# Third attention layer: head means taken from the weights, one norm for two, and gathers sixteen ahead

## What is computed

```python
x = x + _L2_xattn_ref(_layernorm(x, axis=-1), ctx_2048, ...)
...
ln_out = _ln(hidden_states, ln_w, ln_b)
q = _ln(fp8_linear(ln_out, wq, ...).reshape(b, s, g, hpg, d), qln_w, qln_b)   # 16 heads; qx likewise
k = _ln(fp8_linear(ln_out, wk, ...).reshape(b, s, g, d), kln_w, kln_b)        # 8 heads; kx from cond
v = fp8_linear(ln_out, wv, ...)                                               # no norm
core, xout = _gqa(q, k, v), _gqa(qx, kx, vx)
return (concat(core, xout) / smooth, rounded to fp8) @ wproj.T * scales
```

## Time and profile before

| what | value |
|---|---|
| median of 3 runs | 1890.64 us (1887.36 to 1892.12) |
| profiled execution | 1887.24 us, span 1885.5 us, mean PE clock 0.871 |
| busy in the span | PE 1544.3, DVE 1120.1, ACT 813.7, POOL 777.2 us |
| stages touched | l1f 601 to 868, its norms to 883, l2q to 922, main loop to 1350, l3f 1632 to 1885.5 |
| rows put back in l3f | first gather 1678.63, last scatter 1853.75 |

### The profile page before, as it was taken

How to read it: one execution, slowest core, us unless ns; L and a number is a source line. 1 busy time by engine, 2 the same in 40 slices (tenths; PEclk the granted TensorE clock), 3 DMA queues, 4 the chain that set the end, 5 groups by cost and what they waited for, 6 DMA issues and landing times. The chain is left out here.

```text
span 1885.5 us, 25460 instructions
## 1 busy us (share of the span) xinstructions
PE 1544.3 (82%) x8600; PEld 982.3 (52%) x8600; DVE 1120.1 (59%) x2581; ACT 813.7 (43%) x1887; POOL 777.2 (41%) x1038
## 2 busy tenths in 40 slices
PE   6566659999797899994499999999699989837772
PEld 5322225656464455653266676666556565525551
DVE  5999971223674533426789999999622255463335
ACT  2898863110333211113488888888521112412221
POOL 1276641000200497800578777777310000026772
PEclk9666558999697999997699999999799988858886
DMA  2298871110504013111100000000111100146646
GB/s 76 59 180 180 177 153 44 34 42 17 179 2 163 34 56 120 56 45 46 45 1 1 2 1 1 1 2 1 43 29 39 37 24 1 69 177 214 244 140 239
DMA packets 174225, 140.13 MB, mean 74 GB/s; under 512 B 141793, under 2 KB 154721, under 8 KB 170386
## 3 DMA queue, kind: packets, MB, share of 16 engines
q1 hardware_dynamic: 165314, 114.89, 21.4%
q0 software_dynamic: 6416, 22.03, 3.5%
q10 hardware_dynamic: 2368, 1.61, 0.3%
HBM read 85.43 MB, written 19.50 MB: 56 GB/s over the span
## 5 line engine op out<-in xcount | busy, mean ns | idle before, releaser
L1817 POOL CAST l0m_pi<-l0m_pf 128x1024 bf16<-128x1024 int16 x128 | 133.2, 1040 | 111.1 <-ACT l0m_pf L1884 109.6
L1420 PE MATMUL l2x_pr<-l_w,l2x_xq 128*128 128x512 bf16 x576 | 141.4, 384 | 40.0 <-ACT credits L42 40.0
L350 PE MATMUL l1e_gu<-x_normT,l1e_w 128*128 128x512 f32 x384 | 171.6, 601 | 0.0
L1884 ACT ACTIVATE l0m_pf<-l0m_s,l0m_bias,l0x_sq 128x1024 int16<-128x1024 f32 x128 | 153.9, 1204 | 18.7 <-DVE l0m_bias L1915 12.3
L1911 DVE TENSOR_REDUCE l0m_mx<-l0m_s 128x1 f32<-128x1024 f32 x128 | 155.5, 1215 | 5.5 <-PE l0m_s L1826 5.2
L1555 DVE TENSOR_SCALAR l2x_raw<-l2x_raw,l2x_mv,l2x_rs 128x128 f32<-128x128 f32 x384 | 141.7, 429 | 1.6 <-POOL l2x_rs L1399 1.5
L1826 PE MATMUL l0m_s<-l0x_kT,l0x_qT 64*128 64x512 bf16 x256 | 69.0, 559 | 68.5 <-ACT l0m_pf L1884 65.7
L350 PE MATMUL l0e_gu<-x_normT,l0e_w 128*128 128x512 f32 x272 | 121.2, 600 | 0.0
L350 PEld LDWEIGHTS l1e_gu<-x_normT,l1e_w 128*128 128x128 f32 x384 | 74.0, 194 | 84.3 <-issue 83.3
L350 PE MATMUL l2e_gu<-x_normT,l2e_w 128*128 128x512 f32 x256 | 114.5, 602 | 0.0
L426 DVE TENSOR_TENSOR l1e_h<-l1e_sil,l1e_gu 128x512 f32<-128x512 f32 x40 | 27.5, 686 | 133.0 <-ACT l1e_sil L402 133.0
(11 more groups left out here) (516 smaller groups left out, 3562.8 us busy)
## 6 DMA issues: line engine op xcount, KB each, us to landing
l3m_w<-in_l_moe SPq DMA_DIRECT2D x16, 1280.0 KB, 6.4
l1e_w<-in_l_ffn SPq DMA_DIRECT2D x24, 384.0 KB, 3.0
l_rows<-zero_row SPq DMA_DIRECT2D x8, 1024.0 KB, 11.0
l_w<-l_rows SPq DMA_DIRECT2D x8, 1024.0 KB, 11.8
l0e_w<-in_l_ffn SPq DMA_DIRECT2D x17, 384.0 KB, 3.0
l2e_w<-in_l_ffn SPq DMA_DIRECT2D x16, 384.0 KB, 3.1
ctx_tok<-l_route SPq DMA_DIRECT2D x8, 512.0 KB
l2q_wps<-in_l_wp SPq DMA_DIRECT2D x16, 256.0 KB, 2.8
```

The source lines that it names most:

```text
L350: last = nc.tensor.matmul(gu[half][:, m, :], w[:, c % SW, (2 * k + m) * P:(2 * k + m + 1) * P], pg.xnT[:, k, cols(n)], start=(k == 0), sto ...
L1420: last = nc.tensor.matmul(flat(pr[t % 2][:]), src[:, k, tokens], pg.l2_w3[:, part, k, at:at + W], start=(k == 0 and part == 0), stop=(k == ...
L1817: nc.gpsimd.tensor_copy(pi[:, n % 8, :], pf[:, n % 4, :]).then_inc(s["rounded"], 1)
L1884: nc.scalar.activation(pf[:, n % 4, :], s_ps[n % 3][:], ACT.Exp, scale=sq[:, b, h:h + 1], bias=bias[:, n % 4:n % 4 + 1], accum_out=sm[:, b ...
```

## The change

1. **Means out of the weights.** A head's mean over its 128 columns is linear in the weights, so the mean is taken from the weights once. In l1f, DVE runs a new function `beside` behind the multiplications of a chunk. In chunks 0 to 5 and 12 to 15 it sums 8 heads of a 128x1024 piece of `l2_raw` (a reduction) and divides by 128, into `l2_means`; from chunk 12 on it waits for the reload. In chunks 16 and 18 it does the same for the context's weights `l2_wx` and subtracts as well (128x1024). POOL's `l2_split` waits for each mean and scales with eight 128x128 operations that subtract and multiply, where it had one of 128x1024 that multiplied; V keeps the one.
2. **One norm for two.** `l2xm` goes; `l2xn` transposes and takes the factor of both (var x (1 + eps) + eps²).
3. **Rounding.** The subtraction of `l2q` moves from POOL to DVE.
4. **Main loop.** POOL's chain makes no mean, and its constants are folded: 6 operations and a power where there were 9 and a power. DVE multiplies four heads in one 128x512 product with the reciprocal roots broadcast, where it had four operations of 128x128. `aff` holds a factor sqrt(128) for the scales, and is filled by 8 tiny operations, where there were 4.
5. **Gathers.** `AHEAD` becomes 16, in memory that the third attention has left (`spent`); 8 gathers are issued up front, then a scatter and two gathers until 16 are ahead, then one and one, and 16 scatters at the end.

The core of the diff:

```diff
+def l2_centre(pg):
+    v, piece, heads = pg.nc.vector, 1024, 8
+    ch = Chain(None, pg.sem("l2_mean_steps"))
+    def beside(dve, c):
+        ch.eng = dve
+        def mean(dst, rows):
+            ch.link(v.tensor_reduce(dst, rows, AX, ALU.add))
+            return v.tensor_scalar(dst, dst, heads / piece, None, ALU.mult)
+        if c < 6 or 12 <= c < 16:
+            half, (i, k) = (0, divmod(c, KD)) if c < 6 else (1, divmod(c - 10, KD))
+            if half == 0:
+                dve.wait_ge(pg.l2_w_in, 16 * 3)
+            else:
+                dve.wait_ge(pg.l2_rest_in, 16)
+            rows = pg.l2_raw[:, k, i * piece:(i + 1) * piece].rearrange("p (h d) -> p h d", h=heads)
+            mean(pg.l2_means[:, half, k, i * heads:(i + 1) * heads], rows).then_inc(pg.l2_mean_in, 1)
+        elif c in (16, 18):
+            ...
+            ch.link(mean(dst, rows))
+            ch.link(v.tensor_tensor(rows, rows, dst.unsqueeze(2).to_broadcast([P, heads, piece // heads]), ALU.subtract))
+    return beside
...  l2_split
-                    ch.link(g.tensor_scalar(raw, raw, pg.l2_in_scale[:, c:c + 1], None, ALU.mult))
+                    if which == V_:
+                        ch.link(g.tensor_scalar(raw, raw, pg.l2_in_scale[:, c:c + 1], None, ALU.mult))
+                    else:
+                        centred += 1
+                        pool.wait_ge(pg.l2_mean_in, centred)
+                        for h in range(heads):
+                            at_h, m = at + h * P, at // P + h
+                            ch.add(g.tensor_scalar(pg.l2_raw[:, k, at_h:at_h + P], pg.l2_raw[:, k, at_h:at_h + P], pg.l2_means[:, half, k, m:m + 1],
+                                                   pg.l2_in_scale[:, c:c + 1], ALU.subtract, ALU.mult))
+                        ch.wait()
...  ffn_block, DVE, behind the multiplications of a chunk
+                if beside:
+                    beside(dve, c)
...  attention_l2
-    norm(pg, "l2xm", pg.xn)
...  l2q
-            @block.gpsimd
-            def _(pool):
-                for n, (k, j) in enumerate(jobs):
-                    pool.wait_ge(widened, n + 1)
-                    nc.gpsimd.tensor_tensor(xq[:, j, k, :], wide[:, n % 2], step[:, n % 2], ALU.subtract).then_inc(rounded, 1)
...
                     widen(nc, ch, z[:, u], step[:, u], wide[:, u]).then_inc(widened, 1)
+                    dve.wait_ge(widened, n + 1)
+                    nc.vector.tensor_tensor(xq[:, j, k, :], wide[:, u], step[:, u], ALU.subtract).then_inc(rounded, 1)
...  main loop, DVE
-                            for j in range(U):
-                                last = nc.vector.tensor_scalar(raw[:, u, j, :], raw[:, u, j, :], mv[:, u, j, 0:1],
-                                                               rs[:, 1, u, j:j + 1], ALU.subtract, ALU.mult)
-                            last.then_inc(s["normed"], 1)
+                            nc.vector.tensor_tensor(raw[:, u], raw[:, u], rs[:, 1, u].unsqueeze(2).to_broadcast([P, U, DH]), ALU.mult)\
+                                .then_inc(s["normed"], 1)
...  moe_l3
-    GROUP, LOADS, AHEAD, NY = 4, 6, 6, 4
+    GROUP, LOADS, AHEAD, FIRST, NY = 4, 6, 16, 8, 4
...
-            for e in range(AHEAD):
+            for e in range(FIRST):
                 gather(e)
             pool.wait_ge(pg.rows_zeroed, 16 * 8)
             for e in range(E):
                 scatter(e)
-                if e + AHEAD < E:
-                    gather(e + AHEAD)
+                for n in range(min(FIRST + 2 * e, e + AHEAD), min(FIRST + 2 * e + 2, e + AHEAD + 1)):
+                    if n < E:
+                        gather(n)
```

57 lines of the change are left out of this document (30 added, 27 removed).

## The result

The changed kernel takes 1843.41 us in the median of 4 runs (1840.65 to 1846.31), the kernel before 1889.19 in 4 runs beside it (1887.36 to 1892.12). The ratio is 0.9756, interval 0.9733 to 0.978: 46 us faster. The profiled execution took 1841.28 us (span 1839.5, mean PE clock 0.873).

What follows compares the result with a forecast made beforehand. PE was nearly the loop's bound, losing time to waits for DVE and POOL; POOL's indirect DMAs ordered l3f. Terms -15 - 6.5 - 4.6 + 0 - 9 = -35.1 led to 1855 us, own range 1847 to 1867, with rivals 1845 to 1871.

Steps and rivals of the forecast that it cites:

- Norms: Ahead of the main loop: one whole norm of 6.47 us goes, -6.5 us.
- l2q: Rounding ahead of the loop: subtraction on DVE, POOL idle, 35.05 us becomes 30.4, -4.6 us, ends 3.5 and 5.
- l1f: Stage before the norms: DVE's means and POOL's longer split steps fit in beside a busy PE, 0 us.
- the two bounds for the eight operations: POOL's split in l1f: 4.4 us by elements and starts, 7.3 at twice the elements' time; a step 12.9 to 15.8.
- rival C: l1f: POOL's split doesn't fit, ten steps ending too late above 21 us each; slower, 1905 us; 4%.
- l3f: Gathers and scatters: sixteen gathers ahead remove POOL's idle time, -9 us, ends -10 and 0.
- the ring of four outputs: l3f's tail: the last 16 scatters are bound by the experts, 1.63 us each, in four output slots.
- Rival B: l3f's tail: last 16 experts slower than POOL saves, 2.45 us each at lower PE clock, nothing gained, 1864; 12%.
- the term of -15: Main loop: PE's waits for DVE and POOL, 15.8 us, nearly all go; ends -18.5 and -6.
- their hidden part: Main loop: a real wait of PE exceeds the recorded one by 0.16 us, added for 16 and 10 waits.
- Rival A: Main loop gives nothing: product as slow as the four operations, or another engine sets the pace; 1870 us; 17%.
- Rival D: Main loop gives more than the recorded waits, losses over ACT and PE weight loads vanishing too; down to 1846; 7%.

Runs made afterwards that it cites:

- The kernel with two passes: The changed kernel with POOL's eight operations per step of the l1f split made twice, first subtraction, then scaling: 1855.56 us in one profiled run, l1f 290.22.
- The cross of the two: Three variants of the changed kernel: four plain scalings, POOL's chain at ten operations, four operations subtracting a zero mean; 1848.68, 1859.38 and 1873.14 us.
- before again: The kernel before, unchanged, run again: median 1887.51 us, ratio to before 1.0002.
- after again: The changed kernel, unchanged, run again: median 1840.15 us, ratio to before 0.9748.
- the kernel with ten operations and the product: The changed kernel with three more small operations in POOL's chain, result unread, the product kept: 1859.38 us in one profiled run, loop 418.8.

## Why the prediction was right or wrong

**Norms, right.** -6.5 predicted, -6.47 measured (from the norm's first statistics to DVE's first instruction of l2q 14.93 before, 868.23 to 883.16, and 8.46 after, 862.65 to 871.11).

**l2q, right.** A job takes 3.79 where 3.75 and a little for semaphores was reckoned, and the stretch shrinks by 4.52 instead of 4.6.

**l1f, right, with a wrong limit.** The stretch stays at 281.6, PE busy 205 of 205. A step on POOL takes 15.1 to 15.5, within 12.9 to 15.8, by the dearer of the two bounds for the eight operations (6.2 to 7.1 against 4.4 to 7.3). The first half ends at 740.9, the means wait for nothing, POOL ends at 838.7. But rival C's bound for the end, 21 us per step, was wrong: ten steps from 656 to 868 left out the reload, 12.4, and the two steps for V, 11.3 each. With them it is (868 - 656 - 12.4 - 22.6) / 10 = 17.7. The kernel with two passes, at 17.9 and with a slower reload, lost 8.6 us. The margin was some 2 us per step and not 6.

**l3f, right in the sum, wrong in the tail.** -9 was taken, the working gave 9.5, -9.8 was measured. Up to scatter 48, 144.2 us after the first gather (143.9 worked out), POOL had one pause of more than the usual 0.30 us between issues, 0.96 ahead of the first scatter. Behind it I let the ring of four outputs bind at 1.63 us each from expert 52 on. In fact the scatters went on 1.28 apart up to 57, and only the last six came 1.6 apart. Rival B, slow last experts, didn't come: they run at 1.6, not at 2.45.

**Main loop, wrong size and wrong cause.** This is the step that failed: the term of -15 from the marked waits of PE. The sum counted 15.8 and took 15; measured were 19.4, beyond the term's own end of 18.5. Cut at the first projection of the second batch and at that of the eighth, both by the context's weights, the start gave 1.8, six periods 13.1 (305.8 to 292.7), and the end 4.5. At start and end the recorded waits and their hidden part, 5.9 of the 15.8, stand against 6.3 measured. In the six periods they are 9.9, against 13.1: 0.5 us per batch was missing. It is in the timeline of before, in waits that carry no mark:

```profile
983.11 1.05 PE L1433 MATMUL l2x_s<-l2x_kT,l2x_qT 128*128 128x128 f32 x8
984.00 0.60 PE L1440 MATMUL l2x_tr<-ident,l2x_raw 128*128 128x128 f32 x4
...
995.72 1.05 PE L1433 MATMUL l2x_s<-l2x_kT,l2x_qT 128*128 128x128 f32 x8
996.85 0.66 PE L1447 MATMUL l2x_pt<-ident,x_norm 128*128 128x128 f32 x4
997.35 1.46 PE L1420 MATMUL l2x_pr<-l_w,l2x_xq 128*128 128x512 bf16 x6
```

From L1433 to the next group are 1.13 us at 995.72 and 0.89 undisturbed (983.11 to 984.00), and the disturbed group takes 0.50 to the next instead of 0.44. Neither has a bracket. One such gap, 0.24, and some 0.05 behind each of seven disturbed groups, 0.36 in all, make up the half microsecond or so. It was within reach: in after, and in undisturbed batches, PE's period is the sum of its own undisturbed steps, and those could be read in the trace of before: 1.67 at the three marked waits of that batch, 0.24 and 0.36, 2.27 in all, taken from 50.95 leave 48.68. The prediction came to 49.1, from the busy time and the marked waits.

The cause was wrong too. The prediction said that the product takes DVE off PE's way, and that POOL's three operations come on top. The cross of the two shows that neither is worth much alone (-5.2 and +3.2). DVE's share, 92%, and POOL's, 76%, are means over steps; in the steps without a pause both were above PE's 6.09. The 88 us less work on DVE were too much as well: 384 operations at a mean of 429 ns make 1.72 us per four only if they don't overlap, and the same row's busy time, 141.7, makes 1.48. Against the product's 78.3 that is 63 us less, and DVE's busy time in the whole loop fell by 51.6. That the sum came near was luck in so far: it rested on both waits going, and only the pair made them go. Rival A, in which another engine takes DVE's place and sets the pace, is close to what the product alone did: PE waited 0.3 us for DVE at the transposes and 11.4 for POOL.

**Rival D** named losses beyond the recorded waits and down to 1846, and that is what happened in the loop. It got 7%; its mechanism, ACT and weight loads, was not it.

**Untouched stages, not foreseen.** With the touched stretches alone the profiled execution would be 1887.24 - 40.2 = 1847.0, within the range. 5.8 us more came from stages that the change doesn't touch. In the first pair of profiles they lie ahead of l1f's norm (586.66 to 581.07), in the second (before again, after again) behind the loop (328.5 to 321.6), with the start of the kernel slower in after (583.93 to 586.33). Medians agree with some 6 to 7 us in both comparisons (45.8 and 47.4 against 40.2). The sum had no term for these stages, and the range only "some us for the run". Either miss alone, 4.4 us in the loop or 5.8 here, would have left the time inside the range; the two together put it 1.6 below. What makes these stages shorter stays open.

## What to carry to other kernels

Where two helpers feed one engine in turn, read their steps one by one, and count those in which each has no pause: the mean share can hide that both are too slow, and then only relieving both pays. Work taken off one helper can also come back on the other: here 52 us less on DVE put 30 us on POOL. What a bound engine can gain is better found by adding up its undisturbed steps over a period than by adding up its recorded waits. When POOL's issue of indirect transfers is the bound, a gather needs only to be far enough ahead that POOL never waits; what PE then waits for is free.

## What was unexpected of the hardware

- One 128x128 POOL operation with two scalars from memory took 0.79 us in the median of 80, one that subtracts a scalar from memory and multiplies with a constant 1.0 took 0.71, but one that multiplies with 1.0 and with a scalar from memory 0.37 (each the median of 80).
- In the kernel with ten operations and the product, POOL's steps without a pause went from 6.26 to 7.02 us, with the same number and size of operations as before; beside DVE's product they take longer.
- Stages that no edit touched had a few lengths and not one: start to l1f's norm 581 to 582 or 584 to 587 us, l3f's norm to its first gather 43.0 or 46.3, with the granted clock at 0.93 or 0.50 in its second 8 us (both read in two profiles of one kernel). A part of a per cent of such a kernel can thus move without a cause in the code that was changed.
